# Rounding to int16 on ScalarE, widening to bfloat16 on VectorE, in the quantised second phase

## The reference

```python
x = x + _L0_attn_ref(_layernorm(x), ...)          # first phase
# second phase, of z = _layernorm(x), 8192 rows of 512:
x_scale = max(abs(z).max() / 127.0, 1e-5)         # one number over all rows
x_int8 = clip(round(z / x_scale), -128, 127)
acc = x_int8 @ weight_int8.T                      # 512 x 512, exact integers
x = x + acc * x_scale * weight_scale.T + bias
```

## Time and profile before

| | us |
|---|---|
| runs of the kernel before, median of 3 | 1121.34 (1120.61 to 1121.72) |
| the profiled execution, its own time | 1120.91 |
| its span in the profile | 1119.1 |
| TensorE busy in the span | 1071.7 |
| POOL busy | 878.1 |
| DVE busy | 796.8 |
| ACT busy | 697.2 |

### The profile page before, as it was taken

The page is one execution under the profiler, slowest core; times in us unless marked ns, Lnnn a source line. Parts: engine busy times, 40 slices in busy tenths (PEclk is TensorE's granted clock), DMA queues, the critical chain, the costliest instruction groups (busy, mean ns, idle before and its releaser), DMA issues. The chain is left out here.

```text
span 1119.1 us, 30784 instructions
## 1 busy us (share of the span) xinstructions
PE 1071.7 (96%) x11592; PEld 792.0 (71%) x11604; DVE 796.8 (71%) x1529; ACT 697.2 (62%) x1249; POOL 878.1 (78%) x1088
## 2 busy tenths in 40 slices
PE   3889999999999999999999999999999999995998
PEld 1567777777777777777778877777777777762443
DVE  5445667767777777776677667777776777687887
ACT  3566666666566556666566656566666666645996
POOL 4458787777888887888787777888787878883999
PEclk9899999999999999999999999999999999998999
DMA  7222333333333333333333333333323333233994
GB/s 263 57 58 56 88 84 101 88 87 88 91 93 96 94 85 89 86 86 84 93 89 88 87 90 89 88 96 95 96 79 88 92 84 88 51 117 119 372 351 189
DMA packets 73926, 120.80 MB, mean 108 GB/s; under 512 B 16433, under 2 KB 16945, under 8 KB 73778
## 3 DMA queue, kind: packets, MB, share of 16 engines
q1 hardware_dynamic: 72672, 117.24, 35.6%
q10 hardware_dynamic: 1106, 1.58, 0.5%
HBM read 36.97 MB, written 31.46 MB: 61 GB/s over the span
## 5 line engine op out<-in xcount | busy, mean ns | idle before, releaser
L584 PE MATMUL unit<-xt_hi,w_hi 128*128 128x256 f16 x1000 | 275.3, 275 | 12.4 <-DVE w_lo L1295 7.9
L584 PE MATMUL unit<-xt_hi,w_lo 128*128 128x256 f16 x1000 | 275.3, 275 | 0.0
L584 PE MATMUL unit<-xt_lo,w_hi 128*128 128x256 f16 x1000 | 275.3, 275 | 0.0
L906 ACT ACTIVATE relu<-unit,qk_bias_scaled 128x256 f32<-128x256 f32 x250 | 118.0, 472 | 182.7 <-PE unit L584 182.7
L1183 DVE SCALAR_TENSOR_TENSOR x_ring<-sc,x_ring 128x512 f16<-128x512 f32 x256 | 175.4, 686 | 58.2 <-ACT x_ring L948 54.7
L429 POOL TENSOR_TENSOR qk_lo<-f_t,qk_hi 128x512 f16<-128x512 f32 x128 | 149.3, 1167 | 59.0 <-ACT qk_hi L925 59.0
L948 ACT ACTIVATE x_ring<-sc 128x512 f16<-128x512 f32 x256 | 148.1, 591 | 64.5 <-PE sc L630 64.5
L446 POOL TENSOR_SCALAR_AFFINE_SELECT x_ring<-x_ring 128x512 f16<-128x512 f16 x256 | 163.4, 638 | 30.1 <-DVE x_ring L1183 23.4
L448 POOL TENSOR_SCALAR_AFFINE_SELECT x_ring<-x_ring 128x512 f16<-128x512 f16 x256 | 167.4, 654 | 0.0
L584 PEld LDWEIGHTS unit<-xt_hi,w_hi 128*128 128x128 f16 x1000 | 98.6, 99 | 32.1 <-DVE w_lo L1295 8.8
L584 PEld LDWEIGHTS unit<-xt_lo,w_hi 128*128 128x128 f16 x1000 | 98.7, 99 | 17.7 <-issue 0.3
(11 more groups left out here) (211 smaller groups left out, 2741.9 us busy)
## 6 DMA issues: line engine op xcount, KB each, us to landing
stack<-qk_hi SPq DMA_DIRECT2D x504, 64.0 KB, 2.0
xs<-x SPq DMA_DIRECT2D x64, 256.0 KB, 2.7
stack<-qk_lo SPq DMA_DIRECT2D x256, 64.0 KB, 2.0
out<-res SPq DMA_DIRECT2D x64, 256.0 KB, 3.6
x_spill<-xs SPq DMA_DIRECT2D x56, 256.0 KB, 2.1
x_ring<-x_spill SPq DMA_DIRECT2D x56, 256.0 KB, 4.4
stack<-qkv_wt SPq DMA_DIRECT2D x4, 768.0 KB, 9.9
x_ring<-out_wt SPq DMA_DIRECT2D x1, 1024.0 KB, 5.3
```

The lines of the kernel that those rows point to most:

```text
L584: mm = pe.matmul(dst[:, 0:GT], wp[:, k, f:f + P], xp[:, g % 2, k, :], start=(n == 0), stop=(n == len(terms) - 1))
L906: act.activation(relu[:, i % 4, :], src[:, 0:GT], ACT.Relu, bias=qk_bias_scaled[:, f:f + 1]).then_inc(qk_done, 1)
```

## The change

ACT's `scale_tile` writes `u` as int16 in place of float32, so that the write itself converts to an integer, and DVE's `quantise` becomes a plain copy of `u` from int16 to bfloat16. The copy of a round's scales to `cur`, its semaphore and its two waits go, and `scale_tile` reads `affine` of its own round in all rounds. `u` takes half the space. Nothing else changes: the order on each engine, the numbers of buffers and all other waits stay.

```diff
+I16 = mybir.dt.int16
...
-ROUND_MAGIC = 12582912.0
...
-            cur = buf(two, "cur", [P, 2, RING])
...
-            u = buf(two, "u", [P, DEEP, E])
+            u = buf(two, "u", [P, DEEP, E], I16)
...
-            cur_ready = sem("cur_ready")
...
-                def fetch(i, first):
-
-                    if first:
-                        return
-                    act.wait_ge(u_ready, seen(i, -1))
-                    src = affine[:, i] if isinstance(i, int) else affine[:, bass.ds(i, 1)].rearrange("p a s c -> p (a s) c")
-                    act.activation(cur[:, :, :], src, ACT.Copy).then_inc(cur_ready, 1)
-                    act.wait_ge(cur_ready, i)
-
...
-                    own = affine[:, 0] if first else cur
+                    own = affine[:, i]
                     act.activation(u[:, t % DEEP, :], tile_x1(t, last), ACT.Identity, bias=own[:, 1, t:t + 1],
                                    scale=own[:, 0, t:t + 1]).then_inc(u_ready, 1)
...
-                    fetch(i, first)
...
-                    dve.tensor_scalar(xq[:, t % DEEP, :], u[:, t % DEEP, :], ROUND_MAGIC, ROUND_MAGIC, ALU.add, ALU.subtract
-                                      ).then_inc(xq_ready, 1)
+                    dve.tensor_copy(xq[:, t % DEEP, :], u[:, t % DEEP, :]).then_inc(xq_ready, 1)
```

## The result

| | before | after |
|---|---|---|
| median (lowest to highest), us | 1121.58 (1120.61 to 1122.68), 5 runs | 1114.58 (1111.15 to 1116.69), 5 runs |
| profiled execution, its own time | 1120.91 | 1113.27 |
| its span | 1119.1 | 1111.5 |

The medians lie 7.0 us apart, 0.6%; the ratio is 0.9934, with a 95% interval of 0.9918 to 0.9951, so the kernel after is faster. Forecast were 1114.7, range 1113.3 to 1119.0.

The account below looks back on a forecast made before the run. POOL's 1.23 + 0.19 = 1.42 us a tile was taken to bound the second phase; 6.4 us from 58 steps at 1.31 plus 0.2 at the start gave 6.6, so 1121.34 becomes 1114.7 us, range 1113.3 to 1119.0.

Parts of the forecast that it names:

- The bound: Second phase: POOL's residual of 1.23 us plus 0.19 that one `xq` costs it set 1.42 us a tile.
- The cast: DVE's `xq` in the second phase: undisturbed 0.28 us in place of 0.42, 0.15 fixed and the stream halved to 0.13.
- The hold: POOL's 0.19 us loss per `xq` falls to 0.05 (stream less 0.08) or 0.095 (half); pace taken as 1.31 us.
- The start: Start of the second phase: first three `xq` each up to 0.15 us shorter, gain 0 to 0.4 us, taken 0.2.
- ACT: ACT's `u` written as int16 in the second phase: no change from 804 ns, ends 0 and +0.24 us.
- The copies: Three `cur` copies of 222 ns on ACT and their waits: hidden by slack, gain zero, 0.7 us without that cover.
- The transfers: 40 reloading tiles: 400 GB/s at pace 1.31; even a ceiling of 369, with landings of 8.8 us, stays hidden.
- The tail: Behind the last transpose: nothing changes, POOL adds the last four tiles at 1.23 us each, then one store.
- rival 1: POOL's loss in part fixed, not stream: pace 1.33 to 1.38 us, gain 2.4 to 5.3, 1116.0 to 1118.9; chance 0.14.

## Why the prediction was right

- **The bound.** POOL's 1.23 + 0.19 was right for the kernel before, and the runs show what the trace could not: without 0.22 us of TensorE's work the pace stayed at 1.42, with half of POOL's work it fell to 1.30 in the kernel before.
- **The cast.** Forecast 0.28 us; the undisturbed ones take 0.28 (282 ns the shortest). That the stream halves hangs on the 2-byte input; int8 and int32 undo it.
- **The hold.** Of the two ways to scale it, less a fixed overlap (0.05) or by half (0.095), the first was right: 1.28 where it can be seen. That two points fit doesn't show that the mechanism is an overlap of 0.08; no third duration was tried. Having put 1.31 between them I undersized the gain: TensorE's 1.30 binds, 58 steps gave 6.9 us, not 6.4.
- **The start.** 0.2 was taken from between 0 and 0.4; 0.49 came. The first `y` starts 6.22 us behind the first `u` before and 5.81 after, the whole 0.4 of the three shorter `xq`; the last 0.1 came in the next tiles. So 0.49 lies just outside the bounds of the term.
- **ACT.** No price for int16: 804 ns, as forecast. The copies: nothing, in either kernel.
- **The transfers.** 401 GB/s in the stage and reloads landing after 5.0 us in the median, 4.4 before. That lies between no backlog and the 8.8 that a ceiling of 369 would give, and nobody waited for x1. The Trainium skill's about 358 GB/s for such transfers (SBUF — State Buffer, A bandwidth-pool intuition that's wrong (but worth ruling out)) is no ceiling in these runs.
- **The tail.** Nothing: 8.49 and 8.44 us.

The sum was 6.6; the phase gave 7.4 and the medians 7.0. That the forecast of 1114.7 meets the median of 1114.58 to 0.1 us is in part luck: the pace and the start were both undersized, and the same kernel gave a median of 1113.28 in another series. No rival came true. The fixed 0.15 us that rival 1 pointed to is still in the 0.28, but a hold of 0.05 leaves no room for it there.

## What to carry to other kernels

Where POOL and DVE both work out of SBUF, as here, look at the pace of POOL's instructions with and without a DVE instruction of that kind beside them (here at the tail of the phase). The difference is what the DVE instruction costs POOL. It can be part of the bound: here it was 0.19 of 1.42 us a tile, inside durations of POOL that look like work. Two bytes on both sides, int16 into bfloat16 here, shortened it even where the operation stayed the same; int8 didn't. When two chains close at the same pace, take a little work out of one and see whether the pace moves before believing either.

## What I had not expected of the hardware

- The two sides block each other unequally. A short DVE `xq` costs POOL 0.05 us of its 0.28, the long one 0.19 of its 0.42. A POOL residual that had started held a DVE cast for all of its rest (1.35 us for a cast of 0.28), and during a memset of 3.51 us on POOL, which reads nothing, a tensor_scalar of 64 elements lasted 3.52.
- An extra DVE instruction of 0.28 us cost 29 us over 64 tiles, 0.46 a tile, more than its own length: its place against POOL's instructions mattered more than its duration.
